# Graph attention: masks of two chunks as bytes of one 16-bit number, and the halves of V made on GpSimd

## The chip, the cores and the metric

One core of one Trainium2 chip runs the whole program. The metric is the device time of one execution in microseconds. In the text PE is TensorE, DVE is VectorE, ACT is ScalarE, POOL is GpSimd and SP is SyncE, as in the profile.

## The reference

For each of 8 batches, a graph attention layer over 2048 nodes with 256 features each:

```python
h = maximum(layernorm(x), 0)
Wh = h @ W                                  # 2048 x 256
f1, f2 = Wh @ a[:256], Wh @ a[256:]
e = leaky_relu(f1[:, None] + f2[None, :], 0.2)
attention = where(adj > 0, e, -9e15)        # adj: 2048 x 2048 int32
attention = softmax(attention, axis=over i) # over the first index
out = x + elu(attention @ Wh)
```

The softmax runs over the row index i, so one column j of the scores is one softmax. Matrix products are wanted at better than 16-bit precision.

## The kernel before, in words

The columns j are worked on in chunks of 128. There are 16 chunks to a batch and 128 in all, and a chunk c has its column index on the partitions and all 2048 rows i along the free dimension. A step s of the written-out schedule is one turn of the loops `for s in range(...)`, and every engine has its own loop. The order of work on each engine is the order of the calls in that loop; between engines there are only semaphores.

For chunk c the work is:

- POOL starts the DMA `raw <- adj` (line 882), which turns int32 into bf16 on the way. One DMA brings two chunks: 2048 rows as 16 blocks of 128 partitions, 256 columns each.
- DVE turns it into the mask `neg` (`make_mask`, line 762): 0 for an edge and -2^56 for none, 128 x 2048 bf16.
- PE turns the mask over with 16 transposes of 128 x 128 into the PSUM tile `tp` (line 439).
- DVE adds `f1_row` to `tp` and takes the maximum, one custom instruction (`mask_scores`, line 773), into `prob`.
- ACT applies the leaky ReLU (590), makes the negated maximum `shift` (592) and the exponential with its sum (598).
- POOL makes the scaled sum (890), its reciprocal `inv` (893) and the high 16-bit half of the first 1024 rows, `direct` (896). ACT makes the high half of the other 1024 rows, `stored` (604). DVE makes both low halves (787 and 792).
- PE multiplies `direct` with the two halves of `v` at once (lines 504 to 511), and `stored` eight chunks at a time later on (486 to 488).

Beside this, 17 chunks ahead, Wh of chunk c + 17 is made: DVE takes the statistics of x (737, 742), POOL the root (904, once for four chunks) and the normalised `xn` (910), PE transposes it (429), ACT makes `h_t` (610), PE multiplies by W into the PSUM tile `pre` (417). ACT copies f1 and f2 out (579) and writes the high fp16 half of `v` from PSUM (583); DVE writes the low half, `pre` minus the high half (779, `split_v_low`). For chunks below 17, which are made before step 0, `pre` is a bank of `acc`.

Results go through ELU on ACT (646, 651) and DVE (812), and are added to x by a DMA that POOL starts (916).

In step s POOL does, in this order: the three instructions of `split_high(s - 1)`, `xn` of chunk s + 19, the DMA 916 in 8 of 16 steps, the DMA 882 in every second step, and the root in every fourth. DVE does: scores of chunk s, statistics, mask of chunk s + 2, `split_v_low(s + 17)`, then the low halves of chunk s - 1 (787 waits for `direct` from POOL).

Of the kernel before, what the change touches and what calls it, by code (L numbers as in the profile page):

```python
# [11 lines left out]
BF16 = mybir.dt.bfloat16  # L12

# [3 lines left out]
NOT_AN_EDGE = 2.0 ** 56  # L17
# [4 lines left out]
def graph_attention(nc, x, adj, W, a, out):  # L22

# [16 lines left out]
    RF = 20  # L40
# [9 lines left out]
    with ExitStack() as ctx:  # L50
# [23 lines left out]
        h_t = sb("h_t", [P, KC, P], F32)  # L74
        f12 = sb("f12", [P, 64 + RF], F32)
# [18 lines left out]
        minus_half = sb("minus_half", [P, 4], F32)  # L94
        minus_one = sb("minus_one", [P, 1], F32)
        shift = sb("shift", [P, R], F32)
        total = sb("total", [P, R], F32)
        small_total = sb("small_total", [P, R], F32)
        inv = sb("inv", [P, R], F32)
# [8 lines left out]
        raw_in = [sem(f"raw_in{i}") for i in range(2)]  # L108
# [37 lines left out]
        v_ready = sem("v_ready")  # L146
        direct_done = sem("direct_done")
# [190 lines left out]

        finish_index = {item: k for k, item in enumerate(finishing)}
# [4 lines left out]
        def _(sp):  # L344
            def load_x(c):
                if c - RX >= EARLY:
                    sp.wait_ge(xn_ready, c - RX + 1)
# [29 lines left out]
            for c in range(4):  # L377
                sp.dma_start(x_buf(c), x[0, c * P:(c + 1) * P, :]).then_inc(x_early_in[c], 16)
# [29 lines left out]
        def _(pe):  # L408
# [12 lines left out]
            def transpose_x(c):  # L421
# [3 lines left out]
                else:  # L425
                    wait(pe, v_ready, c)
# [121 lines left out]
            for s in range(END + 2):  # L548
# [7 lines left out]
                if chunk(s + 1):  # L556
                    transpose_mask(s + 1)
# [6 lines left out]
        def _(act):  # L564
# [15 lines left out]

            def split_v_high(c):
                wait(act, stored_done, c - RV - 7)
                nc.scalar.copy(v[:, c % RV, 0, :], wh_bank(c)[:, 0:FO]).then_inc(v_hi, 1)

            def attention(c):
# [6 lines left out]
                nc.scalar.activation(shift[:, c % R:c % R + 1], prob[:, c % 2, N:N + 1], ACT.Copy, scale=-1.0  # L592
# [5 lines left out]
                nc.scalar.activation(p, p, ACT.Exp, bias=shift[:, c % R:c % R + 1],  # L598
# [55 lines left out]
            nc.scalar.activation(shift[:, R - 1:R], minus_one[:], ACT.Copy)  # L654
# [8 lines left out]
            for s in range(END + 2):  # L663
# [297 lines left out]
```

## Time and profile before

| | us |
|---|---|
| median of three runs | 992.19 (990.35 to 992.49) |
| the profiled execution, time | 987.88 |
| its span | 986.1 |
| PE busy (matmul) | 950.0 (96%) |
| DVE busy | 920.7 (93%) |
| ACT busy | 879.3 (89%) |
| POOL busy | 645.3 (65%) |

The profiled execution's time holds the span and about 1.8 us around it. Busy time is the union of an engine's instructions; where two instructions of an engine overlap in the record, the second's start tells when the first really let go. Waits are put down to the engine whose semaphore came last. The granted clock of TensorE over the whole span was 0.987 of full speed.

### The profile page before, as it was taken

To read this page: it belongs to the slowest core of one execution; us is meant where nothing else is said; L and a number is where in the kernel's file an instruction comes from. 1 tells how busy PE (TensorE), PEld (TensorE's weight loads), DVE (VectorE), ACT (ScalarE), POOL (GpSimd) and SP (SyncE) were. 2 spreads that over 40 slices of the span, in tenths; PEclk is the share of its full clock that TensorE was granted. 3 is DMA by queue.
4 is the path that set the end of the run, shared out by engine and by line. 5 is a ranking of instruction groups with operands and counts; after the bars stand their busy time and mean duration, and the time that the engine had idled before them with its cause. 6 is when DMAs were issued, how large, how long until landed. Compare 5 with 4: busy or idle time off the path is not lost.

```text
span 986.1 us, 23861 instructions
## 1 busy us (share of the span) xinstructions
PE 950.0 (96%) x8993; PEld 840.0 (85%) x8993; DVE 920.7 (93%) x1271; ACT 879.3 (89%) x1237; POOL 645.3 (65%) x676
## 2 busy tenths in 40 slices
PE   8878999999999999999999999999999999999996
PEld 6666888889888898888888888888988989898896
DVE  8799989999899998999989998999999999999975
ACT  4788989999999999999999899999999999898985
POOL 6567665776766776876767776677676775555540
PEclk8899999999999999999999999999999999999898
DMA  9477667889879889799979988979987978979724
GB/s 233 83 107 108 97 108 122 147 162 156 149 136 176 146 155 167 119 180 149 161 147 144 173 148 151 154 141 172 156 163 123 172 133 138 170 113 158 143 65 140
DMA packets 199093, 142.13 MB, mean 144 GB/s; under 512 B 7361, under 2 KB 187841, under 8 KB 198978
## 3 DMA queue, kind: packets, MB, share of 16 engines
q0 software_dynamic: 140160, 81.80, 61.5%
q1 hardware_dynamic: 58818, 58.81, 20.8%
q8 instruction: 72, 1.18, 0.5%
q14 instruction: 43, 0.35, 0.1%
HBM read 176.16 MB, written 16.84 MB: 196 GB/s over the span
## 4 chain that ended last, share of the span: by engine, by line
POOL 32%; PE 30%; issue 25%; DVE 5%; DMA 4%; ACT 2%; POOLq 0%; SPq 0%; DVEq 0%; ACTq 0%
POOL direct L896 10%; POOL xn L910 6%; POOL raw L882 5%; POOL inv L893 4%; PE acc L511 4%; PE acc L504 4%; PE acc L506 4%; PE tp L439 3%; PE acc_st L486 3%; PE acc_st L487 3%; PE acc_st L488 3%; POOL y L916 3%; PE pre L417 3%; POOL rstd L904 2%; POOL small_total L890 2%
## 5 line engine op out<-in xcount | busy, mean ns | idle before, releaser
L773 DVE CUSTOM_DVE_ANT_0 prob<-tp,f_row 128x2048 f32<-128x2048 bf16 x128 | 292.0, 2282 | 21.5 <-DMA f_row<-f_scratch 14.9
L590 ACT ACTIVATE prob<-prob,f 128x2049 f32<-128x2049 f32 x128 | 257.6, 2013 | 5.4 <-DVE prob L773 5.4
L486 PE MATMUL acc_st<-v,stored 128*128 128x256 f16 x960 | 261.5, 272 | 0.8 <-ACT part L620 0.8
L488 PE MATMUL acc_st<-v,stored 128*128 128x256 f16 x960 | 261.7, 273 | 0.0
L487 PE MATMUL acc_st<-v,stored 128*128 128x256 f16 x960 | 261.6, 273 | 0.0
L598 ACT ACTIVATE prob<-prob,shift 128x2048 f32<-128x2048 f32 x128 | 256.5, 2004 | 4.0
L896 POOL TENSOR_TENSOR direct<-prob,inv 128x1024 f16<-128x1024 f32 x128 | 243.5, 1902 | 10.0
L504 PE MATMUL acc<-v,direct 128*128 128x256 f16 x1024 | 233.4, 275 | 5.4 <-ACT z_direct L626 3.5
L506 PE MATMUL acc<-v,direct 128*128 128x256 f16 x1024 | 233.3, 274 | 0.0
L890 POOL TENSOR_SCALAR small_total<-total 128x1 f32<-128x1 f32 x128 | 29.8, 233 | 272.8 <-ACT prob L598 271.4
L604 ACT ACTIVATE stored<-prob,inv 128x1024 f16<-128x1024 f32 x128 | 146.1, 1142 | 47.6 <-POOL inv L893 47.6
L787 DVE SCALAR_TENSOR_TENSOR direct<-prob,inv,direct 128x1024 f16<-128x1024 f32 x128 | 162.0, 1266 | 12.2 <-POOL direct L896 12.1
L792 DVE SCALAR_TENSOR_TENSOR stored<-prob,inv,stored 128x1024 f16<-128x1024 f32 x128 | 163.7, 1279 | 0.1
L439 PE MATMUL tp<-ident_b,neg 128*128 128x128 bf16 x2048 | 136.1, 220 | 6.1 <-DVE prob L773 6.1
L439 PEld LDWEIGHTS tp<-ident_b,neg 128*128 128x128 bf16 x2048 | 125.4, 98 | 12.1 <-issue 9.2
L511 PE MATMUL acc<-v,direct 128*128 128x256 f16 x1024 | 133.6, 274 | 0.0
L762 DVE TENSOR_SCALAR neg<-raw 128x2048 bf16<-128x2048 bf16 x128 | 129.9, 1015 | 0.8 <-DMA raw<-in_adj 0.8
L417 PE MATMUL pre<-w_cat,h_t 128*128 128x258 f32 x444 | 117.8, 388 | 4.6 <-ACT h_t L610 4.1
L504 PEld LDWEIGHTS acc<-v,direct 128*128 128x128 f16 x1024 | 100.9, 99 | 17.7 <-ACT z_direct L626 4.9
L487 PEld LDWEIGHTS acc_st<-v,stored 128*128 128x128 f16 x960 | 93.7, 98 | 22.0
L506 PEld LDWEIGHTS acc<-v,direct 128*128 128x128 f16 x1024 | 100.9, 99 | 12.0
L910 POOL TENSOR_SCALAR xn<-x_in,rstd,offset 128x256 f32<-128x256 f32 x108 | 107.3, 994 | 5.4 <-DVE offset L755 3.0
(94 smaller groups left out, 1383.9 us busy)
## 6 DMA issues: line engine op xcount, KB each, us to landing
raw<-in_adj POOLq DMA_DIRECT2D x64, 1024.0 KB, 11.2
y<-in_x SPq DMA_DIRECT2D x63, 256.0 KB, 3.1
out<-y SPq DMA_DIRECT2D x63, 256.0 KB, 2.2
y<-elu POOLq DMA_DIRECT2D x56, 256.0 KB, 5.0
x_in<-in_x SPq DMA_DIRECT2D x108, 128.0 KB, 3.3
f_row<-f_scratch SPq DMA_DIRECT2D x31, 256.0 KB, 6.5
stored<-in_x SPq DMA_DIRECT2D x4, 512.0 KB, 6.9
f_scratch<-f_t SPq DMA_DIRECT2D x124, 0.5 KB
```

The lines of the kernel that those rows point to most:

```text
L439: last = nc.tensor.transpose(tp_b[:, m * P:(m + 1) * P], neg[:, c % 2, m, :], ident_b[:])
L486: nc.tensor.matmul(bank[:, 0:FO], p_st[:, 0, rows], v_c[:, 0, :], start=(c == 0), stop=False)
L487: nc.tensor.matmul(bank[:, 0:FO], p_st[:, 0, rows], v_c[:, 1, :], start=False, stop=False)
L488: last = nc.tensor.matmul(bank[:, 0:FO], p_st[:, 1, rows], v_c[:, 0, :], start=False, stop=(c == G - 1))
L504: nc.tensor.matmul(acc[:, m, :], p_d[:, 0, rows], v_c[:, 0, :], start=(j == 0 and m % 2 == 0), stop=False, skip_group_check=True)
L506: nc.tensor.matmul(acc[:, m, :], p_d[:, 0, rows], v_c[:, 1, :], start=False, stop=False, skip_group_check=True)
L511: last = nc.tensor.matmul(acc[:, m, :], p_d[:, 1, rows], v_c[:, 0, :], start=False, stop=(j == C - 1), skip_group_check=True)
L590: nc.scalar.activation(p_top, p_top, ACT.Prelu, bias=f2, alpha=ALPHA).then_inc(leaky, 1)
L598: nc.scalar.activation(p, p, ACT.Exp, bias=shift[:, c % R:c % R + 1], accum_out=total[:, c % R:c % R + 1]).then_inc(prob_ready, 1)
L773: nc.vector.tensor_tensor_reduce(out=prob[:, c % 2, 0:N], in0=tp_b, in1=f1_row[:, b % 2, :], scale=1.0, scalar=-3.0e38, op0=ALU.add, op1=A ...
L896: nc.gpsimd.tensor_tensor(direct[:, c % 2, 0, :], p[:, 0:HALF], k.to_broadcast([P, HALF]), ALU.mult).then_inc(hi_direct, 1)
L910: nc.gpsimd.tensor_scalar(xn_buf(c), x_buf(c), rstd[:, c % RS:c % RS + 1], offset[:, c % RS:c % RS + 1], ALU.mult, ALU.add).then_inc(xn_re ...
```

## The change

The edits, in the order of the work:

- **Masks as bytes.** The two chunks of a pair are now the even and the odd columns of 256 columns (before: the first and the last 128), and a block of 256 rows likewise goes to the partitions two rows at a time. `raw` has four slots. DMA n brings, for the pair n // 2, all even rows (n even) or all odd rows (n odd) of its 256 columns. `make_masks(n)` reads this as 128 x 2048 bf16 and writes 128 x 2048 unsigned bytes, 192 for no edge, without gaps. Two bytes side by side, one of each chunk, are one 16-bit number of `neg`, and 16 transposes per pair of chunks (no longer per chunk) turn these numbers. `mask_scores` reads the bytes of its chunk from `tp` with a step of two bytes, subtracts f1 scaled by 2^-48, and multiplies by -2^48. DVE makes mask n = s + 3 in step s.
- **Rows of x and y.** Their partitions follow the same numbering, (p t) for (t p). Sizes are the same; the two rows of y that a partition holds are now adjacent in memory.
- **V.** ACT copies Wh from PSUM to `wh_sb` in fp32 (`keep_wh`, one buffer). POOL makes both halves from it (`split_v`): a copy to fp16 and a subtraction, after `split_high(s - 1)`. This holds for chunks from 17 on; those before step 0 are made as before. PE's transposes of x wait for `wh_kept` in place of `v_ready`.
- **DMA starts.** POOL starts one raw DMA of 512 KB in each step, in place of one of 1024 KB in every second.
- Small columns are packed into the tile `cols`, and fewer of them are kept.

```diff
-NOT_AN_EDGE = 2.0 ** 56
+F1_SCALE = 2.0 ** -48
+NOT_AN_EDGE = 192.0
...
-        raw = sb("raw", [P, 2, C, 2 * P], BF16)
+        raw = sb("raw", [P, 4, G, 2 * P], BF16)
         neg = sb("neg", [P, 2, C, P], BF16)
+        neg_bytes = neg[:].rearrange("p b m j -> p b (m j)").bitcast(U8).rearrange("p b (t q j) -> p b t q j", t=2, q=G)
...
+        wh_sb = sb("wh_sb", [P, FO], F32)
...
+        tp_bytes = tp[:].rearrange("p h c -> p (h c)").bitcast(U8).rearrange("p (i t) -> p t i", t=2)
...
+        def masks_at(s):
+
+            if s < 0:
+                return [s + 5] if s >= -5 and s < -3 else []
+            return [2, 3] if s == 0 else ([s + 3] if s + 3 < CH else [])
...
-                    wait(pe, v_ready, c)
+                    if c == LEAD + 1:
+                        pe.wait_ge(v_ready, LEAD)
+                    pe.wait_ge(wh_kept, c - LEAD)
...
-            def transpose_mask(c):
-                pe.wait_ge(neg_ready, c + 1)
-                if c == 0:
+            def transpose_masks(pair):
+                pe.wait_ge(neg_ready, 2 * pair + 2)
+                if pair == 0:
                     pe.wait_ge(ident_ready, 1)
-                wait(pe, scores, c)
+                wait(pe, scores, 2 * pair)
                 for m in range(C):
-                    last = nc.tensor.transpose(tp_b[:, m * P:(m + 1) * P], neg[:, c % 2, m, :], ident_b[:])
+                    last = nc.tensor.transpose(tp_b[:, m * P:(m + 1) * P], neg[:, pair % 2, m % 2 * G + m // 2, :],
+                                               ident_b[:])
...
-                if chunk(s + 1):
-                    transpose_mask(s + 1)
+                if chunk(s + 1) and s % 2 == 1:
+                    transpose_masks((s + 1) // 2)
...
+            def keep_wh(c):
+                act.wait_ge(v_ready, c)
+                nc.scalar.copy(wh_sb[:], wh_bank(c)[:, 0:FO]).then_inc(wh_kept, 1)
...
-                    split_v_high(s + LEAD)
+                    keep_wh(s + LEAD)
...
-            def make_mask(c):
-                pair = c // 2
-                dve.wait_ge(raw_in[pair % 2], 16 * (pair // 2 + 1))
-                wait(dve, tp_ready, c - 1)
-                nc.vector.tensor_scalar(neg[:, c % 2], raw[:, pair % 2, :, c % 2 * P:(c % 2 + 1) * P], 0.0, -NOT_AN_EDGE, ALU.is_le, ALU.mult
-                                        ).then_inc(neg_ready, 1)
+            def make_masks(n):
+                pair, t = divmod(n, 2)
+                dve.wait_ge(raw_in[n % 4], 16 * (n // 4 + 1))
+                wait(dve, tp_ready, pair - 1)
+                nc.vector.tensor_scalar(neg_bytes[:, pair % 2, t], raw[:, n % 4], 0.0, NOT_AN_EDGE,
+                                        ALU.is_le, ALU.mult).then_inc(neg_ready, 1)
...
-                    out=prob[:, c % 2, 0:N], in0=tp_b, in1=f1_row[:, b % 2, :], scale=1.0, scalar=-3.0e38,
-                    op0=ALU.add, op1=ALU.max, accum_out=prob[:, c % 2, N:N + 1]).then_inc(scores, 1)
+                    out=prob[:, c % 2, 0:N], in0=tp_bytes[:, c % 2, :], in1=f1_row[:, b % 2, :], scale=-1.0 / F1_SCALE,
+                    scalar=-3.0e38, op0=ALU.subtract, op1=ALU.max, accum_out=prob[:, c % 2, N:N + 1]).then_inc(scores, 1)
...
-                if chunk(s + 2) and s >= 0:
-                    make_mask(s + 2)
+                for n in masks_at(s):
+                    make_masks(n)
...
-                if chunk(s + LEAD) and s != -1:
+                if s < -1 and chunk(s + LEAD):
...
-            def load_raw(pair):
-                wait(pool, neg_ready, 2 * pair - 2)
+            def load_raw(n):
+                pair, t = divmod(n, 2)
+                wait(pool, neg_ready, n - 3)
                 b, q = divmod(pair, C // 2)
-                nc.gpsimd.dma_start(raw[:, pair % 2], adj[b].rearrange("(c p) j -> p c j", p=P)[
-                    :, :, 2 * P * q:2 * P * (q + 1)]).then_inc(raw_in[pair % 2], 16)
+                nc.gpsimd.dma_start(raw[:, n % 4], adj[b].rearrange("(q p t) j -> t p q j", p=P, t=2)[
+                    t, :, :, 2 * P * q:2 * P * (q + 1)]).then_inc(raw_in[n % 4], 16)
...
+            def split_v(c):
+                pool.wait_ge(wh_kept, c - LEAD + 1)
+                wait(pool, stored_done, c - RV - 7)
+                if c == LEAD:
+                    pool.wait_ge(v_ready, LEAD)
+                nc.gpsimd.tensor_copy(v[:, c % RV, 0, :], wh_sb[:]).then_inc(v_hi, 1)
+                pool.wait_ge(v_hi, c + 1)
+                nc.gpsimd.tensor_tensor(v[:, c % RV, 1, :], wh_sb[:], v[:, c % RV, 0, :], ALU.subtract
+                                        ).then_inc(v_ready, 1)
...
+                if s >= 0 and chunk(s + LEAD):
+                    split_v(s + LEAD)
...
-                if s % 2 == 0 and s >= 0 and chunk(s + 4):
-                    load_raw(s // 2 + 2)
+                if s >= -1 and chunk(s + 5):
+                    load_raw(s + 5)
...
-                if s == -16:
-                    load_raw(0)
-                if s == -12:
-                    load_raw(1)
+                if s in (-16, -15, -12, -11):
+                    load_raw((-16, -15, -12, -11).index(s))
```

The order of the instructions changes in two places that matter below. On POOL, in the middle of a batch, one step, from `split_high` to the root. Before (lines 890, 893 and 896 are `split_high`, 910 is `xn`, 882 the raw DMA):

```order
L890 TENSOR_SCALAR small_total<-total 128x1
L893 TENSOR_TENSOR inv<-small_total,minus_one 128x1
L896 TENSOR_TENSOR direct<-prob,inv 128x1024
L910 TENSOR_SCALAR xn<-x_in,rstd,offset 128x256
L882 DMA raw<-in_adj 128x16x256
L904 TENSOR_TENSOR rstd<-var_eps,minus_half 128x4
```

After (910, 913 and 916 are now `split_high`, 924 and 926 `split_v`, 940 `xn`, 902 the raw DMA):

```order
L910 TENSOR_SCALAR cols<-cols 128x1
L913 TENSOR_TENSOR cols<-cols 128x1
L916 TENSOR_TENSOR direct<-prob,cols 128x1024
L924 CAST v<-wh_sb 128x256
L926 TENSOR_TENSOR v<-wh_sb,v 128x256
L940 TENSOR_SCALAR xn<-x_in,rstd,offset 128x256
L902 DMA raw<-in_adj 128x8x256
L934 TENSOR_TENSOR rstd<-var_eps,cols 128x4
```

Two instructions stand between `direct` and `xn`, and the raw DMA, half as large, comes in every step.

On DVE, in the middle of a batch. Before, from the scores of one chunk to the low halves of the chunk ahead of it:

```order
L773 ISA prob<-tp,f_row 128x2048
L773 ISA prob 128x1
L737 BN_STATS stats<-x_in 128x6
L742 BN_AGGR mv<-stats 128x2
L762 TENSOR_SCALAR neg<-raw 128x2048
L779 TENSOR_TENSOR v<-pre,v 128x256
L787 SCALAR_TENSOR_TENSOR direct<-prob,inv,direct 128x1024
L792 SCALAR_TENSOR_TENSOR stored<-prob,inv,stored 128x1024
```

After (796 are the scores, 785 is the mask, 810 and 815 are the low halves):

```order
L796 ISA prob<-tp,f_row 128x2048
L796 ISA prob 128x1
L760 BN_STATS stats<-x_in 128x6
L765 BN_AGGR mv<-stats 128x2
L785 TENSOR_SCALAR neg<-raw 128x2048
L810 SCALAR_TENSOR_TENSOR direct<-prob,cols,direct 128x1024
L815 SCALAR_TENSOR_TENSOR stored<-prob,cols,stored 128x1024
```

Between the mask and the first of the low halves stands nothing any more, but for the small transpose of f1 in every fourth step.

## Rows read from the trace of the kernel before

**Rows 1.** Three stretches: length, busy PE, PEld, DVE, ACT, POOL, granted clock, DMA share, GB/s:

```profile
60.00:90.00 30.00, 22.87 (x204) 17.93 (x204) 28.94 (x41) 25.76 (x36) 21.56 (x22) 1.00 0.64 98
90.00:834.00 744.00, 737.92 (x7105) 658.02 (x7103) 715.45 (x973) 690.02 (x973) 519.67 (x529) 1.00 0.87 148
834.00:949.00 115.00, 109.53 (x1107) 97.79 (x1106) 106.50 (x103) 103.66 (x112) 61.93 (x66) 0.97 0.79 133
```

**Rows 2.** The score instruction (line 773): count, duration min/median/max, first and last start:

```profile
L773 DVE CUSTOM_DVE_ANT_0 prob<-tp,f_row x128: 2269/2278/2293, 32.1 to 949.0; 128x2048 f32<-128x2048 bf16 x128
```

**Rows 3.** Order of time on PE (start us, us): mask transposes, then x:

```profile
302.69 1.06 PE L439 MATMUL tp<-ident_b,neg 128*128 128x128 bf16 x16
303.58 0.39 PE L429 MATMUL pre<-ident,xn 128*128 128x128 f32 x2
```

**Rows 4.** Order of time on ACT, window 300 to 330: first copy of each step:

```profile
300.33 0.14 ACT L579 COPY f<-pre 128x2 f32<-128x2 f32 x1
...
307.50 0.16 ACT L579 COPY f<-pre 128x2 f32<-128x2 f32 x1
...
313.23 1.15 ACT L604 ACTIVATE stored<-prob,inv 128x1024 f16<-128x1024 f32 x1 [0.76 <-POOL inv L893]
```

**Rows 5.** Order of time on DVE, window 300 to 345:

```profile
324.47 1.27 DVE L792 SCALAR_TENSOR_TENSOR stored<-prob,inv,stored 128x1024 f16<-128x1024 f32 x1
...
326.67 2.27 DVE L773 CUSTOM_DVE_ANT_0 prob<-tp,f_row 128x2048 f32<-128x2048 bf16 x1
...
329.57 0.68 DVE L762 TENSOR_SCALAR neg<-raw 128x2048 bf16<-128x2048 bf16 x1
...
330.50 1.27 DVE L787 SCALAR_TENSOR_TENSOR direct<-prob,inv,direct 128x1024 f16<-128x1024 f32 x1
331.70 1.27 DVE L792 SCALAR_TENSOR_TENSOR stored<-prob,inv,stored 128x1024 f16<-128x1024 f32 x1
...
335.88 1.54 DVE L762 TENSOR_SCALAR neg<-raw 128x2048 bf16<-128x2048 bf16 x1
```

**Rows 6.** Order of time on POOL, window 300 to 345:

```profile
324.69 1.97 POOL L904 TENSOR_TENSOR rstd<-var_eps,minus_half 128x4 f32<-128x4 f32 x1
...
334.01 0.23 POOL L890 TENSOR_SCALAR small_total<-total 128x1 f32<-128x1 f32 x1 [2.45 <-ACT prob L598]
334.32 0.58 POOL L893 TENSOR_TENSOR inv<-small_total,minus_one 128x1 f32<-128x1 f32 x1
334.98 1.90 POOL L896 TENSOR_TENSOR direct<-prob,inv 128x1024 f16<-128x1024 f32 x1
336.86 0.99 POOL L910 TENSOR_SCALAR xn<-x_in,rstd,offset 128x256 f32<-128x256 f32 x1
337.80 1.26 POOL L882 DMA_DIRECT2D raw<-in_adj  x1
341.44 0.23 POOL L890 TENSOR_SCALAR small_total<-total 128x1 f32<-128x1 f32 x1 [2.38 <-ACT prob L598]
```

**Rows 7.** All engines in order of time, window 160 to 168: POOL inside two DVE instructions:

```profile
163.15 1.60 POOL L910 TENSOR_SCALAR xn<-x_in,rstd,offset 128x256 f32<-128x256 f32 x1
...
163.19 1.28 DVE L787 SCALAR_TENSOR_TENSOR direct<-prob,inv,direct 128x1024 f16<-128x1024 f32 x1 [0.25 <-POOL direct L896]
...
164.40 1.42 DVE L792 SCALAR_TENSOR_TENSOR stored<-prob,inv,stored 128x1024 f16<-128x1024 f32 x1
```

**Rows 8.** Groups of instructions: shapes, count, busy us, mean ns, idle before:

```profile
L762 DVE TENSOR_SCALAR neg<-raw 128x2048 bf16<-128x2048 bf16 x128 | 129.9, 1015 | 0.8 <-DMA raw<-in_adj 0.8
...
L882 POOL DMA_DIRECT2D raw<-in_adj x64 | 83.5, 1305 | 0.0
...
L916 POOL DMA_DIRECT2D y<-elu x56 | 52.1, 930 | 0.0
...
L779 DVE TENSOR_TENSOR v<-pre,v 128x256 f16<-128x256 f32 x111 | 45.7, 412 | 6.5 <-ACT v L583 6.5
```

**Rows 9.** Who waited for whom: us in total, times, longest:

```profile
POOL small_total L890 <- ACT prob L598: 271.4, 114, 4.6
```

More of the change, by code:

```diff
@@ L12 @@
 BF16 = mybir.dt.bfloat16
+U8 = mybir.dt.uint8
 P = 128
@@ L39, in graph_attention @@
     RV = 34
-    RF = 20
+    RF = 18
     RX = 6
@@ L93, in graph_attention @@
         offset = sb("offset", [P, RS], F32)
[L94 to L99, printed above, removed]
+        cols = sb("cols", [P, 16], F32)
+        minus_half, minus_one, small_total = cols[:, 0:1], cols[:, 1:2], cols[:, 2:3]
+        shift, total, inv = cols[:, 4:6], cols[:, 8:12], cols[:, 12:16]
         acc = psum("acc", [P, NB, FO], F32)
@@ L105, in graph_attention @@
         tp_b = tp[:].rearrange("p h c -> p (h c)").bitcast(BF16)
+        tp_bytes = tp[:].rearrange("p h c -> p (h c)").bitcast(U8).rearrange("p (i t) -> p t i", t=2)
         acc_banks = acc[:].rearrange("p (h m) o -> p h (m o)", m=2)
-        raw_in = [sem(f"raw_in{i}") for i in range(2)]
+        raw_in = [sem(f"raw_in{i}") for i in range(4)]
         x_in_s = [sem(f"x_in_s{i}") for i in range(RX)]
@@ L146, in graph_attention @@
         v_ready = sem("v_ready")
+        wh_kept = sem("wh_kept")
         direct_done = sem("direct_done")
@@ L337, in y_buf, with x_rows @@
             return y[:, k % RY, 0:width(k) // FO, :]
+        def x_rows(c):
+            b, j = divmod(c, C)
+            q, t = divmod(j, 2)
+            return x[b, 2 * P * q:2 * P * (q + 1), :].rearrange("(p t) f -> t p f", t=2)[t]
+        def masks_at(s):
+            if s < 0:
+                return [s + 5] if s >= -5 and s < -3 else []
+            return [2, 3] if s == 0 else ([s + 3] if s + 3 < CH else [])
         finish_index = {item: k for k, item in enumerate(finishing)}
@@ L591, in attention @@
                 act.wait_ge(leaky, c + 1)
-                nc.scalar.activation(shift[:, c % R:c % R + 1], prob[:, c % 2, N:N + 1], ACT.Copy, scale=-1.0
+                nc.scalar.activation(shift[:, c % 2:c % 2 + 1], prob[:, c % 2, N:N + 1], ACT.Copy, scale=-1.0
                                      ).then_inc(shift_s, 1)
@@ L597, in attention @@
                 wait(act, total_s, c - R + 1)
-                nc.scalar.activation(p, p, ACT.Exp, bias=shift[:, c % R:c % R + 1],
+                nc.scalar.activation(p, p, ACT.Exp, bias=shift[:, c % 2:c % 2 + 1],
                                      accum_out=total[:, c % R:c % R + 1]).then_inc(prob_ready, 1)
@@ L653, in _ @@
             act.wait_ge(const_ready, 1)
-            nc.scalar.activation(shift[:, R - 1:R], minus_one[:], ACT.Copy)
+            nc.scalar.activation(shift[:, 1:2], minus_one, ACT.Copy)
             scale_w()
@@ L708, in multiply_w @@
                 nc.vector.tensor_tensor_reduce(
-                    out=w_a[:, i, :], in0=w_raw[:, k, :], in1=a_row[:, side, :], scale=1.0, scalar=0.0,
+                    out=w_a[:, i, :], in0=w_raw[:, k, :], in1=a_row[:, side, :], scale=(F1_SCALE, 1.0)[side], scalar=0.0,
                     op0=ALU.mult, op1=ALU.add, accum_out=w_cat[:, k, FO + side:FO + side + 1]).then_inc(w_ready, 1)
@@ L866, in _ @@
             nc.gpsimd.memset(ident[:], 0.0).then_inc(memset_done, 1)
-            nc.gpsimd.memset(minus_half[:], -0.5)
-            nc.gpsimd.memset(minus_one[:], -1.0)
+            nc.gpsimd.memset(minus_half, -0.5)
+            nc.gpsimd.memset(minus_one, -1.0)
             nc.gpsimd.memset(ones, 1.0)
@@ L887, in split_high @@
                 k = inv[:, c % R:c % R + 1]
-                t = small_total[:, c % R:c % R + 1]
+                t = small_total
                 pool.wait_ge(prob_ready, c + 1)
@@ L903, in root @@
                 rs = slice(chunks.start % RS, chunks.start % RS + len(chunks))
-                nc.gpsimd.tensor_tensor(rstd[:, rs], var_eps[:, rs], minus_half[:, 0:len(chunks)], ALU.pow
+                nc.gpsimd.tensor_tensor(rstd[:, rs], var_eps[:, rs], minus_half.to_broadcast([P, len(chunks)]), ALU.pow
                                         ).then_inc(rstd_s, 1)
```

29 lines of the change are left out of this document (12 added, 17 removed).

## The prediction

> **What bounds the kernel now.** I read the page's busy shares first (PE 96%, DVE 93%, ACT 89%), then the stretches: from 90 to 834 us, where the steps are all alike, PE is busy 99%, DVE 96%, ACT 93% and POOL 70% of the time at full granted clock [rows 1]. The score instruction runs once a step, 128 times from 32.1 to 949.0 us, so a step is 916.9 / 127 = 7.22 us [rows 2]. Three engines are full to within a few per cent, and I work out for each how short its step could be.
>
> PE: the 16 mask transposes hold it from 302.69 to 303.58, 0.89 us a step [rows 3].
>
> ACT: one step goes from 300.33 to 307.50 without a gap, 7.17 us with an ELU in it. The next, without, ends with the high half of `stored` at 313.23 + 1.15 = 314.38, 6.88 us after 307.50, and in it ACT waits 0.76 us for POOL's `inv` [rows 4]. Half the steps are of each kind: ACT can't go below about 7.03 us.
>
> DVE: 715.45 us in 744 us, so 715.45 / 744 x 7.22 = 6.94 us of work per step [rows 1].
>
> POOL: it is the one with room. It waits 2.45 and 2.38 us at its first instruction of a step for ACT's exponential [rows 6], 271.4 us in 114 waits [rows 9]. From that instruction to the end of `direct` takes 334.01 to 336.88, 2.87 us [rows 6].
>
> **How DVE and POOL hold each other up.** Their rows have two lengths. A mask on DVE takes 0.68 us at 329.57, but 1.54 at 335.88, where it ends 0.54 us after POOL's `direct` does (336.88) [rows 5, 6]; its mean is 1.015 us [rows 8]. POOL's `xn`, started at 336.86, lasts until 337.85, 0.43 us after that mask's end at 337.42 [rows 5, 6]: it stood still until the mask was over and needed some 0.44 us itself. The same happens behind the low halves. An `xn` started at 163.15 took 1.60 us, of which 0.35 lie after 164.40, when DVE went on to the next low half; and that next one took 1.42 in place of 1.27 us [rows 7, 5]. A root at 324.69 ended 326.66, 0.92 us after the low half it lay under (325.74) [rows 5, 6]. So one waits for the other's whole instruction, and at a boundary the waiting one gets in.
>
> A rule of the Trainium skill bears on this (SBUF — State Buffer, Who interferes with whom): the pair of ports shared by DVE and GpSimd is locked for an instruction in a two-port mode, and a DVE instruction with two SBUF inputs contends with GpSimd's reads alone. By that rule `direct`, writing and reading, and the new copy and subtraction, which read, all count; the rows above agree for the mask and for both low halves.
>
> **Part by part.**
>
> 1. Transposes. 16 per pair in place of 16 per chunk: 0.89 us less in every second step, so PE's own step falls from 7.22 to about 7.22 - 0.45 = 6.78. This shows in the time only where PE alone sets the step. In steps 112 to 127 nothing of the V work remains and PE is busy 109.53 of 115 us [rows 1]: 16 x 0.445 = 7 us gained there. Elsewhere ACT's 7.03 would be late next.
>
> 2. DVE loses the low half of V, 111 x 0.412 = 45.7 us [rows 8], 0.41 a step. The subtraction stands on POOL now. ACT's copy is of the same size from the same PSUM tile: nothing, and it is covered no differently than before.
>
> 3. The mask writes bytes. No row shows that. Between the mask's 0.68 us (four elements per cycle of the scores' rate, which take 2.28 us for 2048 elements) and 2.28 us [rows 5, 2], I take half of 2.28, 1.14 us: the input is as before, the output no longer of its width, so I expect the fastest rate to go but not both doublings. DVE's work is then 6.94 - 0.41 + 0.46 = 6.99 us a step, or 6.53 and 8.13 at the ends, with the mask's present waits in it.
> The Trainium skill has a rule here (VectorE: DVE Perf Modes, What auto-detection actually checks): the fourfold mode wants 16-bit elements on both sides, the twofold mode with two ports takes any type in SBUF. By its table of tiers that is 1227 ns for 2048 elements; the sum would be 0.09 us a step higher. The scores read bytes with a step of two, from PSUM, where their rate is already one per cycle: nothing, and at most a little.
>
> 4. POOL's starts of the raw DMA: 1.305 us for 1024 KB, 0.93 us for the 256 KB of `y <- elu` [rows 8]. A start of 512 KB is between them; I take 1.1 us. In each step that is 1.1 against 0.65. The DMAs bring the same bytes in rows of the same length, and a buffer is still asked for two steps ahead: nothing.
>
> 5. `split_v` on POOL. The copy of 256 columns costs what `xn` does when it is not held, 0.44 us. The subtraction lies between that and a quarter of `direct` (0.48) with one more start (0.23, as `small_total`): 0.44 to 0.71; I take 0.55. What matters is where they stand. DVE's first low half waits for `direct`, so at the moment T when `direct` ends DVE starts with its port-taking instructions, and POOL starts `split_v`.
>
> The step of POOL, from T, with the mask held until T (as at 335.88):
> mask over at 1.1; copy over at 1.1 + 0.44 = 1.55; first low half, held back 0.15, over at 1.1 + 1.27 + 0.15 = 2.5; subtraction over at 2.5 + 0.55 = 3.05; second low half over at 2.5 + 1.2 + 0.15 = 3.85; `xn` over at 3.85 + 0.4 = 4.25. Then the raw DMA 1.1, the y DMA 56 / 111 x 0.93 = 0.47, the root 0.92 / 4 = 0.23, gaps 0.1, and the 2.87 us to the next end of `direct`: 9.0 us.
> With the mask already done before `direct` starts, the copy goes first (0.45), the low half is over at 1.6, the subtraction at 2.15, the second at 2.95, `xn` at 3.35: 8.1 us.
> Which of the two: DVE, after its low halves (2.95 or 3.85), ELU and part sums (0.5), scores (2.2), statistics (0.7), comes to the next mask at 6.35 to 7.25; `direct` starts at 8.1 - 1.9 = 6.2 or 9.0 - 1.9 = 7.1. They meet nearly at once, so both cases occur. I take the middle, 8.55 us.
>
> Before, by the same working: mask 0.6, `xn` 1.04, DMAs 0.65 + 0.47, root 0.23 to 0.5, 2.87: 5.4 us, and 7.22 - 5.4 = 1.8 us of waiting; 271 us over 128 steps is 2.1. The working is right to some 0.3 us.
>
> So **POOL becomes the bound**. The work of `split_v` is in 111 steps: 111 x (8.55 - 7.22) = +148 us. With -7 from the last chunks: 987.9 + 141 = 1129 us on the profiled execution's scale. The median lies 992.19 / 987.88, 0.4%, higher: **1133 us**. With 8.1 and 9.0 for the step it is 1083 and 1183.
>
> **The rivals.**
>
> A. POOL's new work is hardly held up (faster). Unheld it is 2.87 + 0.44 + 0.55 + 0.44 + 1.1 + 0.47 + 0.23 + 0.25 = 6.35 us, under everybody's step. Then ACT sets 7.03, with DVE's 6.99 beside it: 987.9 - 111 x 0.19 - 7 = 960, 964 as a median. For it: sums of busy time alone say so. Against it: [rows 5 to 7], and that DVE has three such instructions in a row just there. It decides if held time is under 0.7 us a step. 10%.
>
> B. POOL is held in part, some 7.4 to 7.9 us a step, since the halves of V slip between DVE's instructions: 1010 to 1070. 12%.
>
> C. The byte mask runs at one element per cycle, 2.28 us (slower, by DVE). It would then perhaps leave POOL its port. DVE: 8.13 less the mask's present wait, 1.015 - 0.68 = 0.33, is 7.8 to 8.0 us a step: 128 x 0.7 = 90, some 1080. 12%.
>
> D. PE loses its clock, as it is busy less of the time. At 1.2 GHz its 6.78 us would be 13.6 and the bound. Against: from 60 to 90 us it was busy 22.87 of 30 us at 1.00 [rows 1], 76%; in the forecast it is 6.78 / 8.55 = 79%. 3%.
>
> E. Within 0.2%, as gains and losses cancel: 3%.
>
> **How the numbers follow.** 60% for the forecast's mechanism, 1083 to 1183. The range of 1015 to 1185 us holds it and C and most of B, and leaves out A, D, E. A measurement of this kernel can tell about 0.2% from no change; faster by more than that 0.10 (A), within it 0.03, slower 0.87.
>
> **What the profile after will show.** If I am right: the wait of `small_total` for ACT's exponential (271 us) is nearly gone, and in its place ACT waits at `stored` for `inv` (over 100 us in sum), while DVE waits for `direct` at the first low half. The copy's and the subtraction's rows are far longer than 0.44 and 0.55 us, 1 to 1.6 us, and `xn` too. PE is under 85% busy, POOL above 90%. The mask's shortest row is 1.1 to 1.2 us. The first step to look at is POOL's wait: if more than 100 us of it is left, the sum in part 5 is wrong, and if the copy and the subtraction last under 0.7 us each, the holding is.

## The result and the profile after

The changed kernel takes 1207.17 us (median of four, 1206.39 to 1207.52) against 992.34 us for the kernel before (median of four): 1.217 times as long, 95% interval 1.2145 to 1.2187. That is 215 us more, on the side forecast, and 22 us above the top of the range. The profiled execution has a span of 1205.5 us.

The page of the kernel after: the span; busy time, share and instructions of each engine; then the busy tenths of PE and POOL and the granted clock in 40 slices.

```profile
span 1205.5 us, 22130 instructions
...
PE 975.0 (81%) x7969; PEld 789.8 (66%) x7969; DVE 1016.2 (84%) x1160; ACT 879.7 (73%) x1237; POOL 1074.3 (89%) x962
...
PE   8567888788887888877788777887787877889897
...
POOL 7699999999999999999999999999999999976740
PEclk9888998999989999899998999989999899999999
```

POOL went from 65% to 89% and is at 90% or more in 33 slices of 40; PE fell from 96% to 81%. Two stretches, with the columns of [rows 1]:

```profile
90.00:1050.00 960.00, 776.54 (x6374) 629.06 (x6373) 809.77 (x885) 699.79 (x987) 920.87 (x796) 0.96 0.71 116
1050.00:1165.00 115.00, 102.60 (x943) 85.11 (x942) 110.63 (x100) 102.57 (x111) 75.86 (x76) 0.99 0.82 135
```

In the first, POOL is busy 920.87 of 960 us, where before it was busy 519.67 of 744 [rows 1]. The copy of V's first half on POOL (count; duration min/median/max in ns; first and last start) gives the length of a step:

```profile
L924 POOL CAST v<-wh_sb x111: 386/392/1456, 40.7 to 1053.1; 128x256 f16<-128x256 f32 x111
```

(1053.1 - 40.7) / 110 = 9.20 us, against 7.22 before [rows 2] and 8.55 forecast.

Who waited for whom (us in total, times, longest):

```profile
ACT stored L627 <- POOL cols L913: 272.9, 115, 6.0
...
DVE direct L810 <- POOL direct L916: 117.8, 73, 3.9
...
POOL cols L910 <- ACT prob L621: 44.9, 24, 4.0
```

POOL's wait for ACT's exponential, 271.4 us [rows 9], is 44.9 us, and ACT, which had some room, waits 272.9 us for POOL's `inv` (line 913; `inv` is now part of the tile `cols`).

Groups of instructions (count, busy us, mean ns, idle before); `direct` is 916, `xn` 940, the halves of V 924 and 926, the reciprocal 913, the scaled sum 910, the root 934, the DMA starts 902 and 946; on DVE the mask is 785 and the second low half 815:

```profile
L916 POOL TENSOR_TENSOR direct<-prob,cols 128x1024 f16<-128x1024 f32 x128 | 259.1, 2024 | 10.0
...
L815 DVE SCALAR_TENSOR_TENSOR stored<-prob,cols,stored 128x1024 f16<-128x1024 f32 x128 | 207.1, 1618 | 0.0
L785 DVE TENSOR_SCALAR neg<-raw 128x2048 uint8<-128x2048 bf16 x128 | 203.1, 1587 | 0.4 <-issue 0.2
L940 POOL TENSOR_SCALAR xn<-x_in,rstd,offset 128x256 f32<-128x256 f32 x108 | 182.3, 1688 | 0.0
...
L926 POOL TENSOR_TENSOR v<-wh_sb,v 128x256 f16<-128x256 f32 x111 | 168.9, 1522 | 9.0
...
L902 POOL DMA_DIRECT2D raw<-in_adj x128 | 139.9, 1093 | 0.0
...
L913 POOL TENSOR_TENSOR cols<-cols 128x1 f32<-128x1 f32 x128 | 107.5, 840 | 10.7
...
L924 POOL CAST v<-wh_sb 128x256 f16<-128x256 f32 x111 | 89.2, 804 | 12.0 <-ACT wh_sb L603 12.0
...
L946 POOL DMA_DIRECT2D y<-elu x56 | 56.2, 1003 | 0.0
L910 POOL TENSOR_SCALAR cols<-cols 128x1 f32<-128x1 f32 x128 | 47.2, 369 | 53.6 <-ACT prob L621 44.9
...
L934 POOL TENSOR_TENSOR rstd<-var_eps,cols 128x4 f32<-128x4 f32 x31 | 34.7, 1120 | 1.1 <-DVE var_eps L772 0.7
```

The subtraction takes 1.52 us in the mean, and its shortest 0.675; the copy 0.80, and its shortest 0.386. How that comes about, on POOL in order of time (start us, us):

```profile
500.54 1.89 POOL L916 TENSOR_TENSOR direct<-prob,cols 128x1024 f16<-128x1024 f32 x1
502.39 1.39 POOL L924 CAST v<-wh_sb 128x256 f16<-128x256 f32 x1
503.85 1.53 POOL L926 TENSOR_TENSOR v<-wh_sb,v 128x256 f16<-128x256 f32 x1
505.37 2.04 POOL L940 TENSOR_SCALAR xn<-x_in,rstd,offset 128x256 f32<-128x256 f32 x1
...
519.41 1.30 POOL L910 TENSOR_SCALAR cols<-cols 128x1 f32<-128x1 f32 x1
```

and on DVE in the same stretch:

```profile
501.18 2.33 DVE L785 TENSOR_SCALAR neg<-raw 128x2048 uint8<-128x2048 bf16 x1
503.44 1.42 DVE L810 SCALAR_TENSOR_TENSOR direct<-prob,cols,direct 128x1024 f16<-128x1024 f32 x1
504.77 1.69 DVE L815 SCALAR_TENSOR_TENSOR stored<-prob,cols,stored 128x1024 f16<-128x1024 f32 x1
506.39 0.68 DVE L835 SCALAR_TENSOR_TENSOR elu<-elu,z_direct 128x512 f32<-128x512 f32 x1
...
519.43 1.24 DVE L785 TENSOR_SCALAR neg<-raw 128x2048 uint8<-128x2048 bf16 x1
```

The mask (501.18, 2.33 us) waits until `direct` ends at 502.43 and runs to 503.51; the copy (502.39) is over at 503.78, 0.27 us behind it. The subtraction (503.85) ends 505.38, after the first low half (504.86). `xn` (505.37) waits for the rest of the second low half and for the ELU (507.07), and ends 507.41. At 519.41 POOL's scaled sum, 0.24 us by itself, meets a mask (519.43 to 520.67) and takes 1.30 us.

### The profile page after: what moved, and what is told of

It is laid out like the page before. It is cut to its first block, busy times and chain, and to the rows that moved or that the text cites. A ratio compares the mean times of both kernels' runs of the same rounds, so it can differ in the third digit from the quotient of the medians.

```text
span 1205.5 us, 22130 instructions
## 1 busy us (share of the span) xinstructions
PE 975.0 (81%) x7969; PEld 789.8 (66%) x7969; DVE 1016.2 (84%) x1160; ACT 879.7 (73%) x1237; POOL 1074.3 (89%) x962
## 4 chain that ended last, share of the span: by engine, by line
POOL 70%; issue 18%; DVE 4%; PE 4%; ACT 2%; DMA 1%; POOLq 0%; SPq 0%; DVEq 0%; ACTq 0%
POOL direct L916 19%; POOL xn L940 11%; POOL raw L902 9%; POOL cols L913 8%; POOL v L924 7%; POOL v L926 7%; POOL cols L910 4%; POOL y L946 3%; POOL rstd L934 2%; DVE prob L796 1%; DVE stored L815 1%; DVE direct L810 1%; DVE neg L785 1%; ACT z_direct L649 1%; PE acc L524 1%
## 5 line engine op out<-in xcount | busy, mean ns | idle before, releaser
L627 ACT ACTIVATE stored<-prob,cols 128x1024 f16<-128x1024 f32 x128 | 146.8, 1147 | 273.1 <-POOL cols L913 272.9
L796 DVE CUSTOM_DVE_ANT_0 prob<-tp,f_row 128x2048 f32<-128x2048 uint8 x128 | 292.0, 2281 | 9.7 <-DMA f_row<-f_scratch 3.9
L810 DVE SCALAR_TENSOR_TENSOR direct<-prob,cols,direct 128x1024 f16<-128x1024 f32 x128 | 175.4, 1370 | 117.8 <-POOL direct L916 117.8
L916 POOL TENSOR_TENSOR direct<-prob,cols 128x1024 f16<-128x1024 f32 x128 | 259.1, 2024 | 10.0
L621 ACT ACTIVATE prob<-prob,cols 128x2048 f32<-128x2048 f32 x128 | 256.3, 2002 | 4.1
L815 DVE SCALAR_TENSOR_TENSOR stored<-prob,cols,stored 128x1024 f16<-128x1024 f32 x128 | 207.1, 1618 | 0.0
L785 DVE TENSOR_SCALAR neg<-raw 128x2048 uint8<-128x2048 bf16 x128 | 203.1, 1587 | 0.4 <-issue 0.2
L926 POOL TENSOR_TENSOR v<-wh_sb,v 128x256 f16<-128x256 f32 x111 | 168.9, 1522 | 9.0
L434 PEld LDWEIGHTS pre<-w_cat,h_t 128*128 128x128 f32 x444 | 79.6, 199 | 99.5 <-ACT h_t L633 91.3
L902 POOL DMA_DIRECT2D raw<-in_adj x128 | 139.9, 1093 | 0.0
L448 PE MATMUL pre<-ident,xn 128*128 128x128 f32 x218 | 44.9, 288 | 97.5 <-ACT wh_sb L603 97.3
```

Source lines behind the costliest of these rows:

```text
L621: nc.scalar.activation(p, p, ACT.Exp, bias=shift[:, c % 2:c % 2 + 1], accum_out=total[:, c % R:c % R + 1]).then_inc(prob_ready, 1)
L796: nc.vector.tensor_tensor_reduce(out=prob[:, c % 2, 0:N], in0=tp_bytes[:, c % 2, :], in1=f1_row[:, b % 2, :], scale=-1.0 / F1_SCALE, scala ...
L902: nc.gpsimd.dma_start(raw[:, n % 4], adj[b].rearrange("(q p t) j -> t p q j", p=P, t=2)[t, :, :, 2 * P * q:2 * P * (q + 1)]).then_inc(raw_ ...
L916: nc.gpsimd.tensor_tensor(direct[:, c % 2, 0, :], p[:, 0:HALF], k.to_broadcast([P, HALF]), ALU.mult).then_inc(hi_direct, 1)
L926: nc.gpsimd.tensor_tensor(v[:, c % RV, 1, :], wh_sb[:], v[:, c % RV, 0, :], ALU.subtract).then_inc(v_ready, 1)
```

## The experiments

They ran in three sets, and beside them the kernel before had medians of 991.46, 992.75 and 991.69 us; each ratio is to the median of its own set. A step is one chunk of 128 columns, as ahead.

### The two halves of the change, each alone

Masks as bytes alone: the edit takes `split_v` and `keep_wh` out of the changed kernel.

```diff
-                    keep_wh(s + LEAD)
+                    split_v_high(s + LEAD)
...
-                if s < -1 and chunk(s + LEAD):
+                if s != -1 and chunk(s + LEAD):
                     split_v_low(s + LEAD)
...
-                if s >= 0 and chunk(s + LEAD):
-                    split_v(s + LEAD)
```

> The changed kernel with both halves of V made as before (high half on ACT, low half on DVE): what is left of the change is the masks as bytes and the raw DMA in each step. Holding theory (POOL's instructions stand still under DVE's mask, low halves and ELU, and this sets the step): POOL's step is then mask 1.1 + xn 0.44 + raw 1.0 + y 0.5 + root 0.3 + 2.87 = 6.2 us, no bound; DVE is, with its 6.94 us + (1.227 - 0.69) = 7.48 us a step, so 1015 to 1035 us. Rival (the slower byte mask is what costs): most of the 215 us stay, over 1150 us.

Measured: 1006.56 us, 1.015 times before (1.0124 to 1.0176), 8 us under the range of 1015 to 1035 and far from the rival's 1150. One stretch, columns as in [rows 1], and two groups:

```profile
90.00:840.00 750.00, 701.21 (x6217) 604.65 (x6215) 736.27 (x967) 681.45 (x964) 601.32 (x574) 1.00 0.87 144
```

```profile
L784 DVE TENSOR_SCALAR neg<-raw 128x2048 uint8<-128x2048 bf16 x128 | 181.4, 1418 | 0.0
...
L901 POOL DMA_DIRECT2D raw<-in_adj x128 | 157.3, 1229 | 0.2 <-POOL xn L939 0.2
```

DVE is busy 98% of the time and PE only 93%: the bound has gone from PE to DVE, and the transposes saved are worth nothing here. This half of the change, the longer mask and the transposes saved together, costs 15 us. The holding is seen in it already: the mask's mean is 1.418 us for 1.21 alone, and the mean start of a raw DMA is 1.229 us, against 1.093 in the whole change.

V on GpSimd alone: the kernel before with `keep_wh` and `split_v` of the change, the same places and waits (and the small columns packed, for room in SBUF).

> The kernel before with V split on GpSimd from the fp32 copy, and the masks as before. Holding theory: mask over at 0.6 after the end of direct, copy at 1.05, first low half at 2.0, subtraction at 2.7, second low half at 3.6, xn at 4.0 to 4.6 behind the ELU, then 0.65 + 0.5 + 0.3 + 2.87: 8.3 to 8.9 us a step, 1115 to 1180 us. Rival (POOL's additional work by itself, 0.39 + 0.68 us, on its room of 2 us): 995 us or less. Rival (mask): 990 us.

Measured: 1113.38 us, 1.1238 (1.1215 to 1.1261): 2 us below the first forecast's range, and far from the rival's 995. So 1.07 us of POOL's own work, less than its room of 2 us, costs 122 us. The two halves alone cost 15 and 122 us, together 215: 78 us are due to their meeting.

### What is POOL held by?

Without the subtraction:

```diff
-                nc.gpsimd.tensor_copy(v[:, c % RV, 0, :], wh_sb[:]).then_inc(v_hi, 1)
-                pool.wait_ge(v_hi, c + 1)
-                nc.gpsimd.tensor_tensor(v[:, c % RV, 1, :], wh_sb[:], v[:, c % RV, 0, :], ALU.subtract
-                                        ).then_inc(v_ready, 1)
+                nc.gpsimd.tensor_copy(v[:, c % RV, 0, :], wh_sb[:]).then_inc(v_ready, 1)
```

> The changed kernel without the subtraction: GpSimd makes the high half of V alone, and PE multiplies with the high half twice, so its work is the same (the low half of V is left out of the result). Holding theory: the subtraction costs its own 0.68 us and the wait for the first low half, and xn then meets the second low half alone; step 9.2 - 1.4 = 7.8 us, about 1050 us (1030 to 1075). Rival (POOL's work by itself): 111 x 0.68 = 75 us less, 1132 us.

As PE multiplies with the high half twice, this kernel's output is not the layer's; it serves the timing alone.

Measured: 1121.48 us (ratio 1.1318, 1.1295 to 1.1341). That is much nearer the rival (1132) than mine (1050), though for another reason than the rival's, as the rows show. The groups of `xn` and the copy:

```profile
L937 POOL TENSOR_SCALAR xn<-x_in,rstd,offset 128x256 f32<-128x256 f32 x108 | 274.3, 2540 | 0.1
...
L924 POOL CAST v<-wh_sb 128x256 f16<-128x256 f32 x111 | 108.7, 979 | 11.4 <-ACT wh_sb L603 11.3
```

`xn` took over the holding: 2.54 us in the mean, against 1.69 (107 of its 108 rows are above 2.4 us). It starts right behind the copy, under the first low half, and is not let in between the two low halves; it runs when both are over. My rule that a waiting instruction gets in at the next boundary was wrong for it. The sum of 1.4 us per step that I expected back became 0.8.

Dummies in place of V's work tell own work, waits for data and holding apart. Both runs make V as before and put two instructions where `split_v` stood, on a spare tile that nobody waits for. In one they read and write, in the other they write only:

```diff
+                nc.gpsimd.tensor_copy(wh_sb[:], wh_sb[:]).then_inc(dummy_s, 1)
+                pool.wait_ge(dummy_s, 2 * s + 2)
+                nc.gpsimd.tensor_tensor(wh_sb[:], wh_sb[:], wh_sb[:], ALU.subtract).then_inc(dummy_s, 1)
```

> Masks alone, and in split_v's place on GpSimd a copy and a subtraction of 256 fp32 columns of a spare tile onto itself: the instructions of split_v by form, but nobody waits for them, and DVE and ACT make V as before. Holding theory: the whole loss of the change comes back though no data depends on it: mask 1.1, copy 1.5, low half, subtraction 3.4, low half 4.2, xn 4.6 to 5.1, then 1.1 + 0.5 + 0.3 + 3.2: 9.2 to 9.8 us a step, 1190 to 1260 us. Rival (the waits for wh_kept, v_ready and the single buffer): near the 1007 us of the masks alone.

Measured: 1206.18 us (ratio 1.2146, 1.2126 to 1.2166), the changed kernel's time to 1 us. No new wait between engines is needed for the loss: two reading instructions at this place on POOL are enough. By themselves they last 0.39 and 0.61 us, 111 us over 111 steps; against the masks alone (1006.56 us) they cost some 200.

```diff
+                nc.gpsimd.memset(wh_16[:, 0:300], 0.0).then_inc(dummy_s, 1)
+                pool.wait_ge(dummy_s, 2 * s + 2)
+                nc.gpsimd.memset(wh_16[:, 0:512], 0.0).then_inc(dummy_s, 1)
```

> Masks alone, and in split_v's place on GpSimd two memsets of a spare tile, 300 and 512 16-bit elements, some 0.4 and 0.6 us by themselves: instructions that write and do not read (nothing of the result depends on them). Holding theory: they wait for the mask at most, xn behind them waits for a low half or two: step 7.9 to 8.9 us, 1080 to 1180 us, and 50 us or more below the run with dummies that read. Rival (POOL's work by itself): the same as that run within 15 us.

Measured: 1142.17 us (ratio 1.1506, 1.1483 to 1.153), 64 us below. The second memset (count; min/median/max; first and last start), then POOL and DVE in order of time:

```profile
L935 POOL MEMSET wh_sb<- x111: 524/1483/1494, 32.8 to 988.3; 128x512 f16 x111
```

```profile
215.29 0.52 POOL L935 MEMSET wh_sb<- 128x512 f16 x1
...
474.54 0.34 POOL L933 MEMSET wh_sb<- 128x300 f16 x1
474.94 1.48 POOL L935 MEMSET wh_sb<- 128x512 f16 x1
476.41 2.53 POOL L948 TENSOR_SCALAR xn<-x_in,rstd,offset 128x256 f32<-128x256 f32 x1
```

```profile
214.98 1.28 DVE L810 SCALAR_TENSOR_TENSOR direct<-prob,cols,direct 128x1024 f16<-128x1024 f32 x1
...
473.52 2.43 DVE L785 TENSOR_SCALAR neg<-raw 128x2048 uint8<-128x2048 bf16 x1
...
476.21 1.27 DVE L810 SCALAR_TENSOR_TENSOR direct<-prob,cols,direct 128x1024 f16<-128x1024 f32 x1
477.40 1.28 DVE L815 SCALAR_TENSOR_TENSOR stored<-prob,cols,stored 128x1024 f16<-128x1024 f32 x1
```

The second memset needs 0.5 us. It is held by the mask (474.94, 1.48 us, over 0.47 us after the mask's end at 475.95), but where it begins under a low half it takes 0.52 (215.29, under the low half from 214.98 to 216.26). All 64 rows of about 1.48 us lie under a mask, and 45 of the other 47 under a low half: writing alone isn't held by an instruction with two inputs. `xn` reads: from 476.41 it waits for both low halves (to 478.68) and ends 478.94. The Trainium skill says the same (SBUF — State Buffer, Who interferes with whom): a DVE instruction with two SBUF inputs contends with GpSimd's reads and not with its writes, one in a two-port mode with both. These runs agree. Own work by itself doesn't predict the time, since the two pairs of dummies, 0.39 + 0.61 and 0.34 + 0.52 us, differ by 0.14 us a step in their own length, 16 us, and by 64 us in the time.

### Is it the place, or is the port full?

The changed kernel with POOL's step in another order: the DMA starts right behind `direct`, V last.

```diff
-                if s >= 0 and chunk(s + LEAD):
-                    split_v(s + LEAD)
-                if chunk(s + LEAD + 2) and s >= 0:
-                    normalise(s + LEAD + 2)
...
                 if s >= -1 and chunk(s + 5):
                     load_raw(s + 5)
+                if chunk(s + LEAD + 2) and s >= 0:
+                    normalise(s + LEAD + 2)
+                if s >= 0 and chunk(s + LEAD):
+                    split_v(s + LEAD)
```

> The changed kernel with GpSimd's step in another order: split_high, y DMA, raw DMA, then xn, then split_v, so that the DMA starts lie beside DVE's low halves and the copy, the subtraction and xn beside its scores. The same instructions. Holding theory: POOL's step falls to 6.45 us and some holding, and DVE (7.1 us) or ACT (7.03 us) sets it: 970 to 1010 us. Rival (POOL's work by itself): the same instructions, so 1207 us as now, within 10.

Measured: 1103.56 us (ratio 1.1135, 1.1113 to 1.1157). The place matters, 104 us for the same instructions, so the rival's 1207 falls. But I had expected 970 to 1010.

```profile
L815 DVE SCALAR_TENSOR_TENSOR stored<-prob,cols,stored 128x1024 f16<-128x1024 f32 x128 | 223.2, 1744 | 0.0
...
L902 POOL DMA_DIRECT2D raw<-in_adj x128 | 177.7, 1388 | 0.0
...
L926 POOL TENSOR_TENSOR v<-wh_sb,v 128x256 f16<-128x256 f32 x111 | 145.8, 1314 | 9.5
...
L940 POOL TENSOR_SCALAR xn<-x_in,rstd,offset 128x256 f32<-128x256 f32 x108 | 112.2, 1039 | 3.4
```

The raw DMA's start now meets the mask (1.39 for 1.09 us), the subtraction the second low half, which is itself held (1.74 for 1.27 us).

Then, in addition, DVE's mask behind its low halves, so that it no longer meets `direct`:

```diff
-                for n in masks_at(s):
-                    make_masks(n)
...
                 if chunk(s - 1):
                     split_low(s - 1)
+                for n in masks_at(s):
+                    make_masks(n)
```

> The run with V last on GpSimd, and DVE's mask moved behind its two low halves. The same instructions. If the shared port is what is full, its users add up to mask 1.13 + low halves 2.4 + ELU 0.3 + eps 0.1 on DVE and direct 1.9 + small and inverse 0.3 + xn 0.45 + copy 0.39 + subtraction 0.68 + root 0.25 on POOL, 7.9 us a step: no order goes below, 1060 to 1110 us. If only the places were bad, this order, in which direct no longer meets the mask, comes under 1030 us.

Measured: 1099.21 us (ratio 1.1072, 1.1055 to 1.109). Two quite different orders end within 5 us. Their steps, from the first to the last copy of V as above, are 8.29 and 8.25 us, just above the 7.9 us that the users of the shared port add up to. The same sum for the kernel before is 7.9 - 0.53 (mask) - 1.07 (V) = 6.3 of its 7.22 us. This speaks for a full port in these two orders; it does not prove that no other order is better. The 7.9 is also an estimate: it counts 0.3 us for the scaled sum and the reciprocal, whose rows last 0.24 + 0.57. And where V stands ahead of `xn`, as in the change, the sum is not what sets the step: V alone has a sum of 7.4 (7.9 - 0.53) and a step of 8.41 us, and the run with the short mask below has some 7.1 and 8.42.

### The long mask with V on GpSimd, and a version that beats both

Here the DMA casts `adj` to bytes, and DVE makes the mask on pairs of bytes as 16-bit numbers. It is right only where `adj` is 0 or 1, as in this case.

```diff
-        raw = sb("raw", [P, 4, G, 2 * P], BF16)
+        raw = sb("raw", [P, 4, G, 2 * P], U8)
...
-                nc.vector.tensor_scalar(neg_bytes[:, pair % 2, t], raw[:, n % 4], 0.0, NOT_AN_EDGE,
-                                        ALU.is_le, ALU.mult).then_inc(neg_ready, 1)
+                nc.vector.tensor_scalar(neg_pairs[:, pair % 2, t], raw_pairs[:, n % 4], -NOT_AN_EDGE, 257.0 * NOT_AN_EDGE,
+                                        ALU.mult, ALU.add).then_inc(neg_ready, 1)
```

On the changed kernel:

> The changed kernel as it is, V on GpSimd, but with the short mask of the run with bytes from the DMA (0.36 to 0.4 us in place of 1.23 us; right for adj of 0 and 1). Open: how much of the 94 us between V alone (1113 us) and the whole change (1207 us) is the long mask that holds GpSimd, and how much the raw DMA start in each step. If the mask: 8.3 us a step as with V alone, + 0.35 for the starts - 0.2 for the still shorter mask = 8.45 us, 1110 to 1140 us. If the mask's length is indifferent to GpSimd: above 1180 us.

Measured: 1117.49 us (ratio 1.1265, 1.1226 to 1.1304). So a mask of 1.21 us costs 90 us more than one of 0.41 once V is on POOL. What the raw DMA's start in each step costs is not separated: this run (1117 us) has it and V alone (1113 us) has not, but V alone also has a longer mask, 0.68 us, and all the transposes. `direct`, the reciprocal and the copy:

```profile
L918 POOL TENSOR_TENSOR direct<-prob,cols 128x1024 f16<-128x1024 f32 x128 | 245.0, 1914 | 10.0
...
L915 POOL TENSOR_TENSOR cols<-cols 128x1 f32<-128x1 f32 x128 | 78.8, 615 | 10.7
...
L926 POOL CAST v<-wh_sb 128x256 f16<-128x256 f32 x111 | 56.5, 509 | 13.8 <-ACT wh_sb L605 13.8
```

They are back to 1.91, 0.62 and 0.51 us from 2.02, 0.84 and 0.80. By the groups' busy times the scaled sum, the reciprocal and `direct` give 56 of the 90 us, and the copy 33.

On the masks alone, V as before:

> Masks alone (V as before, as in the run of the masks alone), with the DMA casting adj to bytes, and DVE's mask made on 16-bit numbers, 1024 of them in place of 2048 elements: 257 x 192 - 192 x pair (right for adj of 0 and 1, as it is here). If DVE's 7.4 us a step was what the masks alone left as the bound, DVE falls to 6.94 - 0.3 = 6.6 us, and ACT's 7.03 us is next: 965 to 985 us, faster than before. Rival: the DMA, whose rows land with 256 bytes in place of 512, is late and DVE waits for raw: over 1000 us.

Measured: **968.45 us**, 0.9755 times before (0.9735 to 0.9775), faster than the kernel before and the changed one, and for `adj` of 0 and 1 only. The mask, and a stretch in the middle:

```profile
L786 DVE TENSOR_SCALAR neg<-raw 128x1024 uint16<-128x1024 uint16 x128 | 103.9, 813 | 0.0
```

```profile
200.00:800.00 600.00, 583.71 (x5217) 507.14 (x5215) 581.18 (x818) 568.25 (x812) 436.19 (x484) 1.00 0.94 121
```

The same edit of the mask is worth 38 us here (1006.56 to 968.45). The mask is still held in the mean (0.813 us, its shortest row 0.408), yet DVE, PE and ACT are all between 94 and 98%. The DMA's shorter rows keep its engines busy 94% of the time, but nobody waits for them to speak of.

Last, the same with the 16 transposes of a pair made twice:

```diff
-                for m in range(C):
+                for m in [*range(C), *range(C)]:
```

> The run with bytes from the DMA, with each of the 16 transposes of a pair made twice (the same numbers to the same place), so PE has its work of before again, and DVE, ACT and GpSimd keep theirs. If the 24 us gained there are PE's transposes: back to 985 to 1000 us. If they came from DVE's shorter mask: 970 us as without.

Measured: 987.39 us (ratio 0.9961, 0.9944 to 0.9979). PE is full again:

```profile
200.00:800.00 600.00, 597.48 (x5761) 533.55 (x5760) 577.85 (x804) 559.81 (x791) 428.58 (x474) 1.00 0.90 118
```

Of the 24 us, 19 are thus PE's transposes, which is what this change was able to give once DVE's mask was short and V stayed where it was. The short mask with V last on POOL was not run, so how low the best order with V on POOL goes stays open.

## Why the prediction was wrong

The mechanism and the side were right: POOL is the bound, held by DVE's instructions on the shared port; the wait of the scaled sum for ACT fell to 44.9 us, `stored` waits 272.9 us for `inv`, and the mask's shortest row is 1.21 us. The subtraction's mean is 1.52 us as forecast; the copy's is 0.80, under the 1 to 1.6 us forecast, since more than half of the copies were not held. POOL is busy 89% of the span, not above 90, and 96% of the long stretch. The size was not right: 9.20 us a step against 8.55, and a time 22 us above the range. The term that failed is the 2.87 us from the scaled sum to the end of `direct`, which was taken over from the trace of before; it measured 3.47 us (point 5).

1. **Transposes: half as many** is right, but the -7 us in the last 17 steps did not come. From 1050 to 1165 us DVE is busy 110.63 of 115 us, as the mask's additional 0.5 us a step took up what PE gave; the 115.6 us from the last copy (1053.1) to the last score instruction (1168.7) stand against 114.1 us before (834.9 to 949.0). Even with a short mask the transposes are worth nothing there: from the score instruction 16 steps before the last to the last one, the run with bytes from the DMA takes 107.2 us, and 106.8 with the transposes made twice (granted clock 0.98 and 1.00); before it was 110.6. My step that PE alone sets the time there was wrong.
2. **DVE's mask at 1.14 us** was 1.21 to 1.23 us where nothing held it. The Trainium skill (VectorE: DVE Perf Modes, The perf-mode tier table) has 1227 ns for 2048 elements in the twofold mode, and this trace agrees. The score instruction kept 2.28 us with bytes of step two.
3. **A DMA start at 1.1 us**: 1.093. The y DMA 1.00 for 0.93, the root 1.12 for 0.92, which I had read from one row as what was left of a root behind a low half.
4. **`split_v` and `xn`**: from the end of `direct` I had 3.35 to 4.25 us. The means are 0.80 + 0.08 + 1.52 + 1.69 = 4.1, the upper case, not the middle. The subtraction's own time is 0.675 (0.55 taken), `xn`'s shortest row 0.547 (0.40 to 0.44 taken), and `xn` often waited for the ELU as well, which my rule on boundaries excluded.
5. **The term that failed most** is one that I left as it was: "the 2.87 us to the next end of `direct`". Its parts are now 0.37 + 0.84 + 2.02 us with three gaps of 0.08, 3.47 us. A mask of 1.23 us on an engine with time to spare runs into the scaled sum, the reciprocal and the start of `direct`; I had let the mask meet `direct` only, and only to DVE's cost. The run with the short mask shows that: the chain is back at 0.27 + 0.62 + 1.91 us, 56 of its 90 us.

The step is 9.20 - 8.55 = 0.65 us too long. The chain gives 0.6 of it and point 4 0.3, less 0.23 by which POOL's records overlap (they add up to 9.05 us a step between the first and the last copy, and cover 8.82). 111 x 0.65 = 72 us, with the 7 us of point 1 79. Missing are 78 us on the profiled execution's scale (1207.33 - 1129), and 74 between the medians, since the changed kernel's median is not 0.4% above its profiled execution as I had assumed.

My check of the working on the kernel before was weaker than it says: its 5.4 us holds only if the 1.04 us of `xn` takes in the mask's 0.6; the terms as they stand add up to 5.9 and leave 1.4 us of waiting against 2.1 measured.

The range took 9.0 as the highest case of the step, but in the rows of before the mask already lengthened the reciprocal (at most 1.09 us), and nothing in the range stood for that.

Of the rivals, A (little holding) falls with the dummies; B (7.4 to 7.9 us a step) and E (no change) fall with the step of 9.20 us; C (mask at one element per cycle) did not occur; in D the clock did go down to 0.96 in the long stretch, but PE was not the bound there and stayed at 81% of the time, so it had no part that shows.

## What to carry to other kernels

Between VectorE and GpSimd, add up not only busy time but the time in which each needs the port that they share. In this case these were, on VectorE, the mask (a tensor_scalar), which held every kind of GpSimd instruction that it met, writing ones and DMA starts too, and the instructions with two SBUF inputs, which held what reads and not what only writes. If this sum comes near a step, moving work to an engine that looks 65% busy can make all later steps slower, and the sum is at best a lower limit: with V ahead of `xn` the steps were 1.0 to 1.3 us above it. An instruction there costs its own time plus that of what it waits under. Lengthening an instruction that holds the port is priced by what it meets: a mask of 1.21 in place of 0.41 us cost 38 us with V on ACT and DVE, and 90 us with V on POOL.

## What was not expected of the hardware

- `xn`, one input and two scalar columns, waited for two low halves in a row, 2.53 to 2.55 us, when it began some 0.3 us into the first low half directly behind the copy (107 of 108 times in the run without the subtraction). Behind a DMA start it mostly got in after the first (502.24 to 503.31 us in the run with V last, the low half ending 502.89), though five times it took 2.26 to 2.27 us. Before the change, directly behind `direct`, it began 0.05 us ahead of the first low half and got in after it all five times (one of them in [rows 7]). What decides that stays open.
- Starting a DMA on POOL is held by a mask: 1.65 to 1.72 us for the raw DMA in place of 0.96 in the run with V last. Under the low halves it kept its length.
- `tensor_scalar` from 16-bit to byte elements ran at 1.21 us for 2048, and from 16-bit to 16-bit at 0.68.
